# TensorE's program of a DLRM kernel written out for all eight chunks, in place of a loop over five of them

## The reference

```
dots  = einsum('bfd,bgd->bfg', bottom_output, bottom_output)      # 2048 x 27 x 27
pairs = dots[:, TRIL_I, TRIL_J]                                   # 351 below the diagonal
x = concatenate([bottom_mlp_output, pairs, 0], axis=1)            # 2048 x 480
for w, b in ((w0, b0), (w1, b1), (w2, b2), (w3, b3)):             # 480-1024-1024-512-256
    x = relu(x @ w.T + b)
y = x @ w_out.T + b_out                                           # 2048 x 1
```

## Time and profile before

| | |
|---|---|
| Median of 3 runs | 543.13 us (541.19 to 544.7) |
| Profiled execution, its time | 541.43 us |
| Its span in the trace | 539.3 us |
| Granted TensorE clock, mean | 0.971 |
| TensorE matmul (PE) busy | 508.7 us, 94% |
| TensorE weight load (PEld) busy | 479.5 us, 89% |
| VectorE, ScalarE, GpSimd busy | 32%, 31%, 25% |
| DMA queue q1 (data) | 52.22 MB, 51.0% of 16 engines' span |
| DMA queue q8 (instructions) | 67 packets, 1.10 MB |

### The profile page before, as it was taken

The page is one execution under the profiler, slowest core; times in us unless marked ns, Lnnn a source line. Parts: engine busy times, 40 slices in busy tenths (PEclk is TensorE's granted clock), DMA queues, the critical chain, the costliest instruction groups (busy, mean ns, idle before and its releaser), DMA issues.

```text
span 539.3 us, 18870 instructions
## 1 busy us (share of the span) xinstructions
PE 508.7 (94%) x7595; PEld 479.5 (89%) x7595; DVE 171.5 (32%) x384; ACT 166.6 (31%) x380; POOL 132.8 (25%) x242
## 2 busy tenths in 40 slices
PE   6786899999999799989999899997999999999998
PEld 5575898999999799978999799997999999999997
DVE  1155635444313432142312333133322443123110
ACT  3245534334212332133222242223321342123112
POOL 1610311213222231212222132221312132223221
PEclk9687999999999999998999899998999999999999
DMA  8987967757665356553574446653565543300000
GB/s 233 240 267 161 251 98 114 137 97 117 101 119 95 59 91 106 121 89 50 91 121 93 69 77 95 115 98 60 85 105 121 91 75 62 68 28 2 1 0 1
DMA packets 281098, 54.00 MB, mean 100 GB/s; under 512 B 265126, under 2 KB 279230, under 8 KB 281022
## 3 DMA queue, kind: packets, MB, share of 16 engines
q1 hardware_dynamic: 279090, 52.22, 51.0%
q10 hardware_dynamic: 1932, 0.61, 0.5%
HBM read 45.71 MB, written 7.09 MB: 98 GB/s over the span
## 4 chain that ended last, share of the span: by engine, by line
PE 84%; DMA 7%; SPq 4%; issue 2%; DVE 1%; ACT 1%; ACTq 0%
PE acc L668 73%; PE gram_ps L626 8%; DMA rows<-in_r_bottom_output_dram 4%; SPq L439 2%; DMA pairs<-blocks 2%; DMA blocks<-grams 1%; SPq L421 1%; PE gram_ps L594 1%; DVE xt L844 1%; PE side_ps L599 1%; ACT h_full L763 1%; PE acc L599 1%; PE side_ps L689 0%; PE side_ps L594 0%; PE side_ps L642 0%
## 5 line engine op out<-in xcount | busy, mean ns | idle before, releaser
L668 PE MATMUL acc<-h_a,w_hi 128*128 128x256 f32 x1152 | 225.5, 289 | 0.0
L668 PEld LDWEIGHTS acc<-h_a,w_hi 128*128 128x128 f32 x1152 | 183.9, 191 | 2.8
L668 PE MATMUL acc<-h_a,w_lo 128*128 128x256 f32 x576 | 158.6, 283 | 0.0
L763 ACT ACTIVATE h_full<-acc,small_t 128x256 f32<-128x256 f32 x175 | 83.4, 477 | 240.7 <-PE acc L668 240.2
L539 POOL TENSOR_TENSOR h_a<-h_full,h_a 128x256 fp32r<-128x256 f32 x96 | 72.3, 753 | 213.0 <-DVE h_a L856 213.0
L668 PE MATMUL acc<-x,w_hi 128*128 128x256 f32 x504 | 107.9, 301 | 15.6 <-issue 11.6
L668 PEld LDWEIGHTS acc<-h_a,w_lo 128*128 128x128 f32 x576 | 110.3, 192 | 0.0
L668 PEld LDWEIGHTS acc<-x,w_hi 128*128 128x128 f32 x504 | 86.0, 201 | 18.2 <-issue 12.4
L668 PE MATMUL acc<-h_b,w_hi 128*128 128x256 f32 x512 | 101.2, 289 | 0.0
L539 POOL TENSOR_TENSOR h_b<-h_full,h_b 128x256 fp32r<-128x256 f32 x64 | 47.3, 739 | 172.4 <-DVE h_b L856 172.4
L668 PEld LDWEIGHTS acc<-h_b,w_hi 128*128 128x128 f32 x512 | 82.2, 191 | 0.9
(11 more groups left out here) (54 smaller groups left out, 179.0 us busy)
## 6 DMA issues: line engine op xcount, KB each, us to landing
rows<-in_r_bottom_output_dram SPq DMA_DIRECT2D x444, 64.0 KB, 2.1
blocks<-grams SPq DMA_DIRECT2D x30, 216.0 KB, 4.0
w_raw<-in_L_rec_w_dram SPq DMA_DIRECT2D x6, 1024.0 KB, 8.0
early_rows<-in_r_bottom_output_dram SPq DMA_DIRECT2D x12, 224.0 KB, 5.8
stage_pairs<-in_L_rec_w_dram SPq DMA_DIRECT2D x1, 1408.0 KB, 11.5
w_raw<-in_L_rec_w_dram SPq DMA_DIRECT2D x2, 512.0 KB, 8.0
mlp_rows<-r_bottom_mlp_output_dram SPq DMA_DIRECT2D x8, 128.0 KB, 3.2
pairs<-blocks SPq DMA_DIRECT2D x8, 126.0 KB
```

The costliest lines, as they stand in the source:

```text
L668: last = nc.tensor.matmul(acc_slot(c, slot), weight(wp, layer, m, k), in_tile(layer, k, xp), start=(k == 0 and n == 0), stop=(k == K_TILES ...
L763: nc.scalar.activation(h_full[:, slot % 2, :], acc_slot(c, slot), ACT.Relu, bias=small_t[:, slot:slot + 1]).then_inc(drained, 1)
```

## The change

TensorE's chunks 1 to 5 are no longer the body of a loop on the engine: the Python loop emits `chunk(c)` for c = 0 to 7, with c a Python integer. The steps of each chunk, their order, and the programs of SyncE, GpSimd, ScalarE and VectorE, with their loops, stay.

```
--- before.py
+++ after.py
@@ -712,11 +712,8 @@
                     turn_weights(step[1])
                 elif step[0] == "mlp":
                     turn_mlp(0)
-            chunk(0)
-            with pe.Fori(1, CHUNKS - 2) as c:
+            for c in range(CHUNKS):
                 chunk(c)
-            chunk(CHUNKS - 2)
-            chunk(CHUNKS - 1)
             out_row(CHUNKS - 1)
```

## The result

The changed kernel takes 524.33 us (median of 4 runs, 524.15 to 526.09), the kernel before 543.10 us (4 runs, 541.19 to 544.7): ratio 0.966, 95% interval 0.963 to 0.970. The forecast was 525.5 us. The profiled execution of the changed kernel took 524.15 us, its span is 522.0 us, 17.3 us shorter than before.

The account below looks back on a forecast made before the run. TensorE was taken to bound the kernel, with 84% of the wait chain. From the profiled 541.43 us, less 12.25 for pauses and 4.26 for slow heads, came 524.9; forecast 525.5 us, range over all cases 523.0 to 530.5.

Parts of the forecast that it names:

- The pauses: TensorE's idle before the first matmuls of chunks 2 to 5, where its loop returns; removing them saves 12.25 us.
- The slow heads: Starts of chunks 3, 4 and 5, run at reduced TensorE clock after idling; expected to vanish, saving 4.26 us.
- The form of the waits: TensorE's waits compare with constants instead of computed register values; taken as 0, bounds 1 us for five chunks.
- Straight-line fetches: TensorE's longer program in chunks 1 to 5 might stall on instruction fetch; taken as 0, up to 7.5 us.
- The other engines' ways back: Jumps to the loop head on SyncE, GpSimd, ScalarE, VectorE; 0.45 us each, all hidden, upper bound 5.5 us.
- the rival in which the pause is handed on: VectorE's or ScalarE's loop return replaces TensorE's pause at chunk starts; 530.4 us, or 535 with three slow heads; chance 6%.
- The median: Whole-run median, 1.7 us above the profiled run before; forecast 524.9 to 526.6 us, set at 525.5.
- Rival 4: Straight-line code starves TensorE at some 40 fetch crossings in chunks 1 to 5; 15 stalls give 547.4 us; chance 2%.

Follow-up runs that it names:

- near loops: Changed kernel plus a tiny three-turn loop in TensorE's program before each of chunks 2 to 5; 528.21 us against 524.33 for the changed kernel.
- moved code: Changed kernel with 24 already fulfilled waits at the head of TensorE's program, moving what follows by 12 instructions; 526.02 us beside 525.58 unmoved.
- two ways back: Changed kernel with TensorE's chunks 1 and 2 as one loop, 3 and 4 as another; 537.83 us, ratio 0.990 to the kernel before.
- the kernel with a pause and no jump: Changed kernel, but TensorE waits at the head of chunks 2 to 5 for VectorE's last step and an added memset; 542.74 us, ratio 1.000 to before.
- two ways back and moved code: Kernel with two TensorE loops of two chunks, plus 48 fulfilled waits at its program's head, moving code by 24 instructions; 534.24 us, ratio 0.982 to before.

## Why the prediction was right

**The pauses** (forecast 12.25 us): all four went, and nothing took their place; chunk 2 to 5 each begin at the very turn of the next matmul. That they were a jump to code that had to be fetched was argued from the place alone. The near loops show that two jumps to code close by cost 0.27 to 0.42 us, the packets show that TensorE starts again 1.61 to 1.75 us after a piece of code has landed, and the moved code shows that a missing piece of code stops TensorE for 2 to 3 us. In the kernel with two ways back, a second wait for code followed seven matmuls behind the first, and moving the code took it away. The Trainium skill, "Runtime: NRT & Kernel Launch", Instruction fetch mechanics, says that a taken branch to code outside what is held makes the engine wait for a fetch, and that crossing from block to block in straight line is mostly hidden; by that rule, the trace agrees in the chunks, and does not before chunk 0, where straight-line code lost 2.18 us at one crossing.

**The slow heads** (forecast 4.26 us): gone, and caused by the pauses, as the kernel with a pause and no jump shows. A pause need not bring one, and which do was not foreseen. That three of four heads were slow in the profiled execution before is what that one execution had. The measured sum of both is 16.87 us where 16.51 was forecast. The difference is the base: I took 58.73 us, chunk 2's work, as a chunk at full clock, and it is 58.64; 58.73 is a chunk behind a pause whose head stays fast (chunk 4 with two ways back and moved code has 58.73 again).

**The form of the waits** (0, bounds 1 us either way): 0. Looped chunks entered without a pause take 58.64 us, as written-out ones do.

**Straight-line fetches** (0, up to 7.5 us): 0 in chunks 1 to 5, five chunks with TensorE busy for 58.64 of 58.64 us.

**The other engines' ways back** (0.45 us each, hidden): hidden. From the branch of a way back to the next instruction of the same engine, the packed trace of the changed kernel has 0.29 to 0.34 us on VectorE, 0.24 to 0.28 on ScalarE, 0.28 to 0.33 on SyncE and 0.16 or 0.17 on GpSimd, so 0.45 was too much. On VectorE, the one with least to spare, this lies under the last step: it is idle for 0.11 us at the start of chunk 2, and with all five engines written out for 0.16 us at the same place. So the rival in which the pause is handed on, which was to give 530.4, was further away than I had it. With TensorE's loop kept and the others written out nothing was gained.

**The median:** 524.33, 1.2 us below the forecast. I had left up to 1.7 us for an offset between median and profiled run; the changed kernel's median lies 0.18 us above its profiled run (524.15), the fastest of the four. In the kernel before, a slow head is worth 1.4 us and may or may not come, which fits its wider spread (538.5 to 546.0 over 23 runs, and one of 546.9); how many heads were slow in the runs without a profile was not seen. That the forecast came so near is in part luck: the stretch before chunk 1, which it took as unchanged, lasted from 118.98 to 122.46 us in the ten profiled executions.

**Rival 4** has a slip: fifteen stalls, 547.4 us, would be 0.8% above the median before and not over 1%; that takes sixteen.

## What to carry to other kernels

A loop on the engine that sets the time costs at each turn what its jump back to unfetched code costs, plus what the clock loses behind the pause: here 4.2 us of 62 a turn with four ways back, and 7.0 or 4.6 a turn in the two kernels with two, part of it by where the loop's head happened to lie and part by how long the clock stayed low. Look for an "issue" wait at the head of each turn but the first and none at the exit, and count the clock's slow stretch behind it in the same sum. What tells a wait for code from one for data is a packet of the instruction queue that starts in each of the pauses, with the engine starting again the same time after each has landed; with the pauses made by a wait for data, one of the four had a packet in it and three had none. Write out only that engine's program; the loops of engines with time to spare cost nothing that could be measured here, and writing them out as well brought nothing.

## What the runs showed of the hardware

- A pause of 2.8 to 3.8 us sometimes leaves TensorE at 2.4 GHz (chunk 2 before, chunk 4 with two ways back and moved code, chunk 3 with the others written out, behind 3.66 us) and sometimes costs 1.4 to 3.6 us of slow clock. Which of these comes was not settled.
- TensorE waits for its own code in straight line too, where it is made of small matmuls only: before chunk 0 the changed kernel lost 3.0 + 2.2 us of "issue" at three places, at each of which it started again 1.3 to 1.6 us after a packet of q8 had landed, and that is the largest thing of this kind left in it.
